# Recurrent weights of a gated recurrent layer: loaded late in 32x32 squares and transposed by VectorE, not TensorE

## What is computed

```
x = x + MoE(x, cond)      # shared: silu(x w1) * (x w3) w2;  8 experts: gelu(x W1e) W2e, the top 2 by sigmoid scores
x = x + GRU(x, h0=cond)   # per time step t, for all 8 sequences:
    Z  = sigmoid(Xz[t] + H Whz.T + bhz);   R = sigmoid(Xr[t] + H Whr.T + bhr)
    Ht = tanh(Xh[t] + (R * H) Whh.T + bhh);  H = Z * H + (1 - Z) * Ht;  Y[t] = H Whq.T + bhq
    with Xz, Xr, Xh = X Wxz.T + bxz, X Wxr.T + bxr, X Wxh.T + bxh
```

## Time and profile before

| | us |
|---|---|
| median of 3 executions (lowest, highest) | 1278.68 (1277.61, 1278.76) |
| the profiled execution, time | 1277.44 |
| its span, first to last instruction | 1275.5 |
| TensorE busy (products, weight loads apart) | 1249.8 |
| VectorE, ScalarE, GpSimd busy | 997.2, 803.3, 7.4 |

### The profile page before, as it was taken

The page is one execution under the profiler, slowest core; times in us unless marked ns, Lnnn a source line. Parts: engine busy times, 40 slices in busy tenths (PEclk is TensorE's granted clock), DMA queues, the critical chain, the costliest instruction groups (busy, mean ns, idle before and its releaser), DMA issues.

```text
span 1275.5 us, 84499 instructions
## 1 busy us (share of the span) xinstructions
PE 1249.8 (98%) x35704; PEld 890.8 (70%) x35704; DVE 997.2 (78%) x6111; ACT 803.3 (63%) x4402; POOL 7.4 (1%) x25
## 2 busy tenths in 40 slices
PE   9999999999999999999999999999999999999887
PEld 8877677766677776667776667776667776666554
DVE  6678888788787888878888787887877787877765
ACT  4366666666666666666666666666666666666554
POOL 1000000000000000000000000000000000000000
PEclk9999999999999999999999999999999999999999
DMA  8211011111101111011111101111011111001110
GB/s 273 57 36 43 24 38 30 42 41 34 36 24 39 38 37 45 24 37 27 44 39 35 38 21 41 35 39 45 27 33 27 44 39 33 23 21 27 33 32 11
DMA packets 76186, 51.34 MB, mean 40 GB/s; under 512 B 40609, under 2 KB 73761, under 8 KB 75809
## 3 DMA queue, kind: packets, MB, share of 16 engines
q1 hardware_dynamic: 75128, 45.29, 13.7%
q10 hardware_dynamic: 680, 0.66, 0.2%
HBM read 29.13 MB, written 16.78 MB: 36 GB/s over the span
## 4 chain that ended last, share of the span: by engine, by line
PE 93%; DVE 3%; ACT 2%; issue 1%; DMA 1%; SPq 0%
PE dn_ps L1083 27%; PE up_ps L1111 26%; PE zc_bank L1247 21%; PE r_bank L1247 14%; PE aux L1083 2%; DVE terms L1006 2%; PE dn_ps L1119 1%; ACT t_h L713 1%; PE misc L1083 1%; DVE hist L1009 1%; DMA x_all<-in_L_cond_W1e 1%; DVE t_rT L982 1%; ACT t_r L693 0%; DVE rhT L985 0%; SPq L411 0%
## 5 line engine op out<-in xcount | busy, mean ns | idle before, releaser
L982 DVE STREAM_TRANSPOSE t_rT<-t_r 128x32 f32<-128x32 f32 x1024 | 156.2, 191 | 171.1 <-ACT t_r L693 163.6
L693 ACT ACTIVATE t_r<-r_bank 128x32 f32<-128x32 f32 x1024 | 146.1, 195 | 210.2 <-PE r_bank L1247 200.2
L713 ACT ACTIVATE t_h<-zc_bank 128x32 f32<-128x32 f32 x1024 | 145.9, 195 | 207.7 <-PE zc_bank L1247 207.7
L1083 PE MATMUL dn_ps<-we_sb,x_all 128*32 128x256 f32 (+1 forms) x5144 | 274.5, 329 | 0.0
L1247 PEld LDWEIGHTS zc_bank<-whT,rhT 128*8 128x8 f32 x8192 | 118.1, 87 | 177.5 <-DVE rhT L985 176.9
L1247 PE MATMUL r_bank<-whT,hist 128*8 128x64 f32 x8192 | 210.1, 220 | 16.0 <-DVE hist L1009 13.4
L1247 PE MATMUL zc_bank<-whT,rhT 128*8 128x64 f32 x8192 | 211.0, 220 | 2.8 <-DVE rhT L985 0.3
L1247 PE MATMUL zc_bank<-whT,hist 128*8 128x64 f32 x8192 | 208.9, 219 | 0.8 <-issue 0.8
L1006 DVE STREAM_TRANSPOSE terms<-t_h 128x32 f32<-128x32 f32 x1024 | 156.5, 192 | 38.2 <-ACT t_h L713 19.7
L1247 PEld LDWEIGHTS r_bank<-whT,hist 128*8 128x8 f32 x8192 | 117.6, 88 | 94.6 <-DVE hist L1009 72.5
L1083 PEld LDWEIGHTS dn_ps<-we_sb,x_all 128*32 128x32 f32 x5144 | 137.9, 110 | 31.9 <-issue 1.0
(11 more groups left out here) (132 smaller groups left out, 1691.4 us busy)
## 6 DMA issues: line engine op xcount, KB each, us to landing
gate_inputs_by_group<-gru_raw SPq DMA_DIRECT2D x64, 192.0 KB, 2.0
gru_raw<-gate_inputs_by_group SPq DMA_DIRECT2D x256, 48.0 KB
xT_all<-in_x SPq DMA_DIRECT2D x448, 8.0 KB
x_all<-in_x SPq DMA_DIRECT2D x31, 128.0 KB
out<-gru_raw SPq DMA_DIRECT2D x31, 128.0 KB
x_all<-in_L_cond_W1e SPq DMA_DIRECT2D x4, 512.0 KB, 7.6
we_sb<-in_L_cond_W2e SPq DMA_DIRECT2D x4, 512.0 KB, 8.6
xT_all<-in_L_cond_w SPq DMA_DIRECT2D x2, 256.0 KB, 5.3
```

Source lines behind the costliest of these rows:

```text
L693: act.activation(t_r[:, i, :], r_ps[:, i * Q:(i + 1) * Q], ACT.Tanh, scale=0.5).then_inc(tr_ready, 1)
L713: act.activation(t_h[:, i, :], c_ps[:, i * Q:(i + 1) * Q], ACT.Tanh, scale=-1.0).then_inc(th_ready, 1)
L982: dve.transpose(t_rT[:, i, :], t_r[:, i, :]).then_inc(trT_done, 1)
L1083: done = pe.matmul(ps[Q * j:Q * (j + 1), col:col + cols], lhsT[:, Q * j:Q * (j + 1)], rhs, start=first, stop=last, tile_position=(0, Q * j ...
```

## The change

SP no longer issues the seven loads between those of the expert weights. Behind the output's bias it issues 12 loads for the three Wx (per matrix four, one for each quarter of the partitions: 32 partitions x 16 runs of 128 bytes), waits for two shared hidden units, and issues 16 loads for the three Wh and Whq (32 partitions x 8 runs of 256 bytes each). `load_late(4)` moves behind the first gate inputs. VectorE turns all squares with 14 transposes of 128x256, two a matrix. TensorE's 28 transposes, the seven moves out of its banks, and GpSimd's eight reordering copies are gone; ScalarE halves Whh in place. `gate_biases` moves behind the first accumulation of tile 1.

```diff
+            def load_blocks(blocks, w, loaded):
+                by_row = w.rearrange("(n r) c -> r n c", r=Q)
+                for j in range(NG):
+                    sp.dma_start(blocks[Q * j:Q * (j + 1), :, :], by_row[:, :, GW * j:GW * (j + 1)]).then_inc(loaded, 16)
+            def load_wx(g):
+                by_row = gru_wx[g].rearrange("(n r) (k c) -> r k n c", r=Q, k=KC)
+                for j in range(NG):
+                    sp.dma_start(wx_blocks[g][Q * j:Q * (j + 1), :, :, :], by_row[:, :, :, Q * j:Q * (j + 1)]).then_inc(ld_wx[g], 16)
...
             load_we1(1)
-            for r, part, _ in WEIGHTS:
-                if part == "x":
-                    load_gru(r, ld_gru_x)
             load_we1(2)
             load_we2(1)
-            for r, part, _ in WEIGHTS:
-                if part != "x":
-                    load_gru(r, ld_gru_h)
...
             sp.dma_start(bias_q[:, :], ...)
+            for g in range(GATES):
+                load_wx(g)
+            sp.wait_ge(shared_ready, 2)
+            for g in range(GATES + 1):
+                load_blocks(wh_blocks[g], gru_wh[g], ld_wh[g])
...
-            load_late(EARLY)
...
             for q in range(PIECES):
                 gate_rows(q, 1, xs_second)
+            load_late(EARLY)
             load_late(EARLY + 1)
...   GpSimd
-            pool.wait_ge(ld_gru_h, LDH)
-            for r, w in ordered.items():
-                for o in range(KC):
-                    pool.tensor_copy(...)
-            pool.wait_ge(tr_done, WEIGHTS_DONE)
+            pool.wait_ge(wx_turned, GATES * KC)
             pool.memset(xs, 0.0).then_inc(xs_zeroed, 1)
...   ScalarE
             consume_up(1, 0)
+            act.wait_ge(wh_turned, GATES * NI)
+            act.activation(whT[:, 2, :, :], whT[:, 2, :, :], ACT.Copy, scale=0.5).then_inc(whh_halved, 1)
             consume_up(1, 1)
...   VectorE
+            def turn_wx(g):
+                dve.wait_ge(ld_wx[g], 16 * NG)
+                for k in range(KC):
+                    dve.transpose(wxT[:, k, :, COLS[g]].rearrange("p j (b r) -> p j b r", r=Q),
+                                  wx_blocks[g][:, k, :, :].rearrange("p (j b) q -> p j b q", j=NG)).then_inc(wx_turned, 1)
+            def turn_wh(g):
+                dve.wait_ge(ld_wh[g], 16 * NG)
+                for i in range(NI):
+                    dst = whT[:, g, i, :] if g < GATES else wqT[:, i, :]
+                    dve.transpose(dst.rearrange("p (n r) -> p n r", r=Q), wh_blocks[g][:, :, Q * i:Q * (i + 1)]).then_inc(wh_turned, 1)
...
                 accumulate(0, e - 1)
+                if e >= NE - 2:
+                    turn_wx(e - NE + 2)
...
             accumulate(0, NE - 1)
-            gate_biases()
+            turn_wx(2)
             accumulate(0, NE)
             accumulate(1, 0)
-            for q in range(PIECES):
-                add_bias(0, q)
+            gate_biases()
+            add_bias(0, 0)
+            turn_wh(0)
+            add_bias(0, 1)
+            turn_wh(1)
+            turn_wh(2)
             shared_silu(1, 0)
             shared_hidden(1, 0)
+            turn_wh(3)
             shared_silu(1, 1)
...   TensorE
+                    if (t, q) == (0, 0):
+                        pe.wait_ge(wx_turned, GATES * KC)      # project
...
             for e in range(NE):
                 unit(0, NSH + e)
-                downs = [(0, e)]
-                for at in range(max(len(ROUND_TR[e]), len(downs))):
-                    if at < len(ROUND_TR[e]):
-                        transposes(m)
...
+                whole_down(0, e)
...
                             pe.wait_ge(seeded_r, 1)
+                            pe.wait_ge(wh_turned, NI * 2)
+                            pe.wait_ge(whh_halved, 1)
```

More of the change, by code:

```diff
@@ L73, in moe_then_gru @@
         gru_raw = sb("gru_raw", [P, 11, KC, C])
-        raw = [gru_raw[:, r, :, :] for r in range(7)]
-        ordered = {r: gru_raw[:, 7 + i, :, :] for i, r in enumerate((1, 3, 5, 6))}
+        RB = C // Q
+        wx_blocks = [gru_raw[:, g, :, :].rearrange("p o c -> p (o c)").rearrange("p (k n q) -> p k n q", k=KC, q=Q) for g in range(GATES)]
+        BLOCK_HOME = 6
+        wh_blocks = [x_all[:, BLOCK_HOME + 2 * g:BLOCK_HOME + 2 * (g + 1), :].rearrange("p n c -> p (n c)").rearrange("p (n c) -> p n c", n=RB)
+                     for g in range(GATES + 1)]
         we2_sb = sb("we2_sb", [P, NE, HE // P, C])
@@ L151, in moe_then_gru @@
         ld_h0 = sem("ld_h0")
-        ld_gru_x = sem("ld_gru_x")
-        ld_gru_h = sem("ld_gru_h")
+        ld_wx = [sem(f"ld_wx{g}") for g in range(GATES)]
+        ld_wh = [sem(f"ld_wh{g}") for g in range(GATES + 1)]
+        wx_turned = sem("wx_turned")
+        wh_turned = sem("wh_turned")
+        whh_halved = sem("whh_halved")
         ld_bias = sem("ld_bias")
@@ L162, in moe_then_gru @@
         consts_ready = sem("consts_ready")
-        ordered_done = sem("ordered_done")
         tr_done = sem("tr_done")
@@ L225, in moe_then_gru @@
         EARLY = 4
-        WEIGHTS = [(0, "x", 0), (2, "x", 1), (4, "x", 2), (1, "h", 0), (3, "h", 1), (5, "h", 2), (6, "q", 0)]
-        WSCALE = {"x": [1.0, 1.0, 1.0], "h": [1.0, 1.0, 0.5], "q": [1.0]}
         HEAD_TR = [("x", 0), ("x", 1), ("cond", 0)]
[L230 to L234, removed]
+        NTR = len(HEAD_TR)
+        gru_wx = [wxr, wxz, wxh]
+        gru_wh = [whr, whz, whh, whq]
         gate_bx = [bxr, bxz, bxh]
         gate_bh = [bhr, bhz, bhh]
-        LDR, LDX, LDH = 16 * 3, 16 * 3, 16 * 4
+        LDR = 16 * 3
         LDB = 16 * (2 * GATES + 1)
@@ L243, in w13_cols @@
             return slice(half * HS // 2, (half + 1) * HS // 2)
-        def in_round(e):
-            sizes = [len(HEAD_TR)] + [len(r) for r in ROUND_TR]
-            return range(sum(sizes[:e + 1]), sum(sizes[:e + 2]))
         def evacuate(m):
-            kind, i = GROUPS[m]
+            kind, i = HEAD_TR[m]
             src = tr_ps[m % 2]
@@ L255, in evacuate @@
                 return xT_all[:, 2 * i:2 * i + 2, :, :].rearrange("p n k t -> p (n k t)"), src[:, 0:512], 1.0
[L256 to L259, removed]
-            if part == "x":
[L261 to L264, removed]
+            return condT[:, :, :].rearrange("p k t -> p (k t)"), src[:, 0:C], 1.0
         def sig(p):
@@ L411, in load_x @@
                     sp.dma_start(x_all[:, n, :], x[:, n * TS:(n + 1) * TS, :]).then_inc(ld_x[i], 16)
-            def load_gru(r, loaded):
-                sp.dma_start(raw[r][:, :, :], gru_w[r].rearrange("(o p) c -> p o c", p=P)).then_inc(loaded, 16)
+            def load_blocks(blocks, w, loaded):
[6 more added lines that the diff above has]
+                    sp.dma_start(wx_blocks[g][Q * j:Q * (j + 1), :, :, :], by_row[:, :, :, Q * j:Q * (j + 1)]).then_inc(ld_wx[g], 16)
             load_x(0, slice(0, 1))
@@ L545, in _ @@
             pool.drain().then_inc(consts_ready, 1)
-            pool.wait_ge(ld_gru_h, LDH)
-            for r, w in ordered.items():
-                for o in range(KC):
-                    pool.tensor_copy(w[:, o, :].rearrange("p (i j c) -> p i j c", i=NI, j=NG),
-                                     raw[r][:, o, :].rearrange("p (j i c) -> p i j c", j=NG, i=NI)).then_inc(ordered_done, 1)
-            pool.wait_ge(tr_done, WEIGHTS_DONE)
+            pool.wait_ge(wx_turned, GATES * KC)
             pool.memset(xs, 0.0).then_inc(xs_zeroed, 1)
@@ L562, in take @@
                 act.activation(dst, src, ACT.Copy, scale=s).then_inc(tr_act, 1)
[L564 to L568, removed]
             def score_tanh(i, tiles):
@@ L672, in _ @@
                     split_we1(e + 3)
-                take_round(e)
                 if e == NE - 2:
@@ L927, in _ @@
                 op()
-            take_round(2)
             for e in range(2, NE):
@@ L931, in _ @@
                     split_we1(e + 2)
-                if e > 2:
-                    take_round(e)
                 accumulate(0, e - 1)
+                if e >= NE - 2:
+                    turn_wx(e - NE + 2)
                 if e == 5:
@@ L1045, in transposes @@
                     blocks = [x_all[:, 2 * i + n, k * P:(k + 1) * P] for n in range(2) for k in range(KC)]
-                elif kind == "cond":
+                else:
                     pe.wait_ge(ld_router, LDR)
                     blocks = [cond_tok[:, k * P:(k + 1) * P] for k in range(KC)]
[L1049 to L1056, removed]
                 for at, blk in enumerate(blocks):
@@ L1191, in output @@
                 if i == 0:
+                    if t == 0:
+                        pe.wait_ge(wh_turned, NI * (GATES + 1))
                     pe.wait_ge(yst_ready, t + 1)
@@ L1298, in _ @@
             early_logits()
-            m = len(HEAD_TR)
             for e in range(NE):
                 unit(0, NSH + e)
-                downs = [(0, e)]
-                for at in range(max(len(ROUND_TR[e]), len(downs))):
-                    if at < len(ROUND_TR[e]):
-                        transposes(m)
```

(4 more changed lines are left out.)

## The result

The changed kernel took 1281.14 us (median), against 1278.82 for the kernel before in the same comparison: ratio 1.0017 [1.001, 1.0024]. It is slower by 2.3 us by the medians and 2.2 by the ratio. The prediction was 1277.4, with a range of 1275.7 to 1281.0, and "no change" as the likeliest verdict with its centre on the faster side. The profiled execution has a span of 1277.7, 2.2 above the 1275.5 of before.

What follows compares the result with a forecast made beforehand. TensorE was taken as the bound, alone on the chain through the head. The terms -3.08 + 0.6 + 1.2 + 0 = -1.3 gave 1276.1 us for the profiled execution, 1277.4 as a median, range 1275.7 to 1281.0.

Steps and rivals of the forecast that it cites:

- The transposes, -3.08: Head: seven groups of four TensorE transposes at 0.44 go, moving everything on TensorE behind them forward by 3.08 us.
- the 0.6: Head, tile 0's accumulation 8: third Wx lands at 36.7, needed at 36.1, so TensorE is 0.6 us late (0 to 3.2).
- Wx's packets at 1000 a us: Head: the three Wx, 6144 packets of 128 bytes, move at 1000 a us and take 6.1 us (5.1 to 7.8).
- A turn at 0.42: VectorE: each 128x256 transpose takes 0.42 us, so 14 add 5.9 us of work at most.
- The stall at expert 3, 1.2: TensorE at expert 3's `down` products: VectorE's accumulation 1 of tile 1 is 1.6 late, slack 0.35, stall 1.2 us.
- Whq's landing: Head: all Wh and Whq landed at 40.8 (37.8 to 44.5), VectorE wanting the last at 44.6; cost 0 at the middle.
- SP itself: ... it is free at 37.6 to 42.9, middle 40.2 ... 0 at the middle: SP's 28 weight issues end before the first gate input store, due at 41.2; cost 0, 1.7 to 2 at far end.
- a tail of 0.04: If each 512-run issue took 1.74, the twelve would end 9 us behind the need: about 1286, chance 0.04.
- TensorE, not the gate inputs, sets the start: 1.3 earlier than before: Scan start: gate inputs land at 47.9, seed 0.65 later, TensorE arrives at 49.6, so the scan starts 1.3 us earlier.
- Tile 4, "just hidden, 0 (0 to 1.1)": In the scan: moved load of tile 4 lands at 61.7, VectorE wants it at 61.5 with 0.36 idle; cost 0.
- the third rival: Tile 4's moved load becomes the wait, landing at 64.8 at worst: 1278.9 half way, 1280.4 at the end; chance 0.15.
- the second: Rival: small-packet loads are late, at turn_wx(2), then at `add_bias` and SP's store: 1280.0 to 1280.7; chance 0.25.

Runs made afterwards that it cites:

- act_wh: The changed kernel with the eight loads of Whh and Whq issued from ScalarE's queue instead of SP's: 1277.96 us, ratio 0.9992 to the kernel before.
- wh_rows: The changed kernel with Wh and Whq in 4 loads of whole 1 KB rows instead of 16, values not the reference's: 1277.89 us, ratio 0.9999.
- tile4_pool_late: The changed kernel with tile 4's 17 loads issued by GpSimd, behind its clearing of `xs`: 1279.7 us, ratio 1.0006 to the kernel before.
- wh_pool: The changed kernel with the 16 loads of Wh and Whq issued early in the head by GpSimd instead of SP: 1284.73 us, ratio 1.0033.
- whq_tile4_turns: The changed kernel with Whq's loads behind the stores, tile 4's issued late by GpSimd, and VectorE's turns of Wh and Whq moved later: 1279.29 us, ratio 1.0003.
- whq_later: The changed kernel with Whq's four loads behind the gate inputs' stores and its turns behind tile 1's accumulations: 1280.54 us, ratio 1.0014.

## Why the prediction was wrong, step by step

All of it can be read as one path through SP's queue. Wherever SP issues tile 4's loads behind the gate inputs and VectorE waits for them, tile 4 is transposed 13.9 to 14.6 us behind ScalarE's first use of the gate inputs (six traces of five kernels; 14.6 in the change). So late gate inputs make tile 4 late by as much, whatever TensorE has gained in the head. The prediction had gate inputs at 47.9 and tile 4 at 61.7; it was 50.51 and 65.09. Of these 3.4 us, 1.3 are the first store's late issue, 1.4 its slow landing, and 0.8 tile 4's own loads (0.1 came back in between).

- **The transposes, -3.08:** right. TensorE transposes tile 0 at 38.20 instead of 40.66, 2.46 earlier (3.00 in the second trace of the change, which was 0.4 further ahead before the first weight transposes); the sum had -3.08 + 0.6. But the 0.6 is there for another reason: Wx was on time, and TensorE waited 0.40 at 25.53 (0.20 in the second trace) for an accumulation of VectorE that its own transposes had covered before. The chain of the earlier trace rows had shown that TensorE never waited; it couldn't show how close to a wait it was.
- **Wx's packets at 1000 a us:** right. From 29 to 33 us, 3911 packets ran, 978 a us.
- **A turn at 0.42:** 0.38 each, right.
- **The stall at expert 3, 1.2:** measured 1.17, but a coincidence. In act_wh and wh_rows, with the same turns and Whq on time, it is 0.27. The other 0.9 is Whq's landing, for which the sum had 0 (the last Whq was there at 45.4, not 40.8: that figure counted packets only, and SP's last issue of Whq ended at 42.48). The stall also cost 1.45 rather than 1.17: TensorE was 2.39 early at 44.30 (46.69 before), and 0.94 early behind the stall.
- **"SP itself: ... it is free at 37.6 to 42.9, middle 40.2 ... 0 at the middle":** this is the step that failed. It was free at 42.5, and the first store went out 1.3 behind VectorE. The 12 issues of 512 runs took 0.85 each on average, with 0.66 in the last four, and the 16 of 256 runs took 0.49; the sum had 0.52 to 0.64 for both. They began at 24.08, in the middle of the range. I took the middle of the two ends, where the case was nearer to the far one: twelve of the issues had eight times the runs of those in the rows that gave 0.52 to 0.64, and I kept that for a tail of 0.04.
- **The landing of the stores** was taken as before, without a term of its own: 3.4 instead of the 2.0 that wh_rows shows. It is known by its size alone; as said at tile4_pool_late, its cause is open. Of the 2.46 between act_wh's gate inputs and the change's, 1.53 is the first store's later issue and 1.14 the rest up to the reading back (45.98 - 42.52 against 43.31 - 40.99); the reading itself gave 0.2 back.
- **"TensorE, not the gate inputs, sets the start: 1.3 earlier than before":** wrong by these two. TensorE was ready at 49.94, the gate inputs at 50.51, and the start was 0.02 earlier.
- **Tile 4, "just hidden, 0 (0 to 1.1)":** it landed 14.6 behind the gate inputs (65.09 - 50.51), inside 12.4 to 15.2 but 0.8 above the middle. It is SP's issues again: 1.32 up to the first, 10.19 for the sixteen (the sum's middle had 9.3), and 3.07 from the last one's start to VectorE's transposition (2.8 to 3.6 in the sum). The bound counted from gate inputs at 47.9; with these at 50.5 the tile was late by 2.30, +1.95 net.

What happened is the third rival, at its far end and a little beyond: it had tile 4 at 64.8, with the long issues and SP's lateness in it, and a time of 1280.4. Of the second only the half on SP's store came true; its other half, the Wx behind 37.9, did not. The two were priced at 0.15 and 0.25 as alternatives, and the corner in which both add up was left out of the range by the text itself. But they have one cause, SP's full queue, and are not independent. The 1.95 lost before step 5 is most of the measured 2.2; the drift of single executions behind it (see the table) is tied to no instruction of the change, and stays open.

## What to carry to other kernels

When loads are cut into small runs, count the queue's issue time against the first thing that must follow them in the same queue, and leave room for a slower landing of the next store; two late transfers behind one queue add up. An idle engine's queue can take the issues for nothing (act_wh), but only if its packets don't go out before others that are wanted sooner (wh_pool). And removing work from the bounding engine uncovers the waits that it hid, so look how long before its use each input was ready, not only whether the engine waited.

## What the runs showed of the hardware

- TensorE's granted clock fell to 0.51 behind a wait of 2.25 (whq_tile4_turns), and step 1 of the scan came 1.26 later for it, 1.45 in whq_later behind a wait of 2.46. Behind waits of 0.85 and 1.18 (the change, twice) and of 1.40 (tile4_pool_late) it stayed at 1.00, and step 1 lost nothing.
- A stall of TensorE at expert 3's `down` products cost 0.27 more than its idle time: 1.45 for 1.17, and 0.54 for 0.27 in act_wh (44.05 against 46.69 before the stall, 47.02 against 49.12 behind it). At the start of the scan it was less, 0.92 for 0.85 (from 49.67, the last `up` product, to 50.79, against 50.61 to 50.81 before).
- An issue of SP took about 0.49 for 256 runs of 256 bytes and 0.66 for 512 runs of 128 (0.85 on average over all twelve of these in the change); ScalarE's issues 0.46, GpSimd's 0.58. So the number of runs counts little, and the number of issues much. Single issues in a long row took far more: one of tile 4's took 1.98 in the change (at 54.20).
- The DMA moved 978 packets of 128 bytes a us at 85.1% of the engines (changed kernel, 29 to 33 us):

```profile
DMA packets 3911, 0.53 MB, mean 132 GB/s; under 512 B 3871, under 2 KB 3910, under 8 KB 3910
...
q1 hardware_dynamic: 3910, 0.52, 85.1%
```
